# A transformer layer with a routed mixture: the second batch's rows are sent two at a time among the expert blocks' transfers

## The reference, cut to what matters

```
x = layernorm(x + attention(x))                     # 2 batches of 1024 tokens, width 128, 16 heads
logits = router(x)                                  # 8 experts
top_logits, idx = top_k(logits, 2); scores = softmax(top_logits)
for e in range(8):
    a, g = split(x_rep @ w1[e].T, 2)                # width 352 each
    he = silu(a) * g @ w2[e].T
    out = out + where(expert_ids == e, he, 0)
combined = (out * scores).reshape(N, 2, 128).sum(1)
x = layernorm(x + combined)
```

## Time and profile before

| what | value |
|---|---|
| median of 3 runs | 865.77 us (865.43 to 865.95) |
| the profiled execution | 863.55 us |
| its span, first to last instruction | 861.8 us |
| PE busy | 765.6 us, 89% |
| ACT busy | 687.8 us, 80% |
| POOL busy | 673.9 us, 78% |
| DVE busy | 537.6 us, 62% |
| mean granted TensorE clock | 0.967 |

### The profile page before, as it was taken

One profiled execution on the slowest core, in us unless ns is written; L12 is line 12 of the kernel. 1 busy time (PEld: TensorE's weight loads), 2 busy tenths in 40 slices (PEclk: granted clock), 3 DMA queues, 4 the chain that ended last, 5 costly groups with the idle time before them and its releaser, 6 DMA issues. The chain is left out here.

```text
span 861.8 us, 22282 instructions
## 1 busy us (share of the span) xinstructions
PE 765.6 (89%) x9183; PEld 525.2 (61%) x9183; DVE 537.6 (62%) x907; ACT 687.8 (80%) x854; POOL 673.9 (78%) x430
## 2 busy tenths in 40 slices
PE   2889999999999999999999999999988657839991
PEld 0346565666666666666666666666655446729990
DVE  6856667666666676666866667766653167515673
ACT  3899999998989898999999898989889755214452
POOL 5799888888888797888898789999999962554441
PEclk9999999999999999999999999999999987959996
DMA  5603064303031211213040404031200041121212
GB/s 174 150 2 75 5 139 82 78 2 78 8 72 27 53 39 41 54 27 75 5 108 5 112 2 111 14 99 39 48 11 17 11 117 44 36 71 51 79 40 86
DMA packets 43138, 49.30 MB, mean 57 GB/s; under 512 B 6785, under 2 KB 27655, under 8 KB 42912
## 3 DMA queue, kind: packets, MB, share of 16 engines
q1 hardware_dynamic: 39872, 43.31, 20.4%
q0 software_dynamic: 2496, 4.24, 1.5%
q10 hardware_dynamic: 672, 0.33, 0.2%
HBM read 14.28 MB, written 9.25 MB: 27 GB/s over the span
## 5 line engine op out<-in xcount | busy, mean ns | idle before, releaser
L882 POOL TENSOR_TENSOR pl<-p,ph 128x1024 f16<-128x1024 f32 x256 | 541.0, 2130 | 70.2 <-ACT ph L784 69.6
L944 DVE TENSOR_REDUCE mx<-mps 128x1 f32<-128x1024 f32 x249 | 303.8, 1220 | 133.7 <-PE mps L619 131.6
L783 ACT ACTIVATE p<-sps,escale 128x1024 f32<-128x1024 f32 x256 | 286.3, 1118 | 51.2 <-PE sps L599 45.6
L784 ACT ACTIVATE ph<-sps,escale 128x1024 f16<-128x1024 f32 x256 | 284.9, 1113 | 0.0
L694 PE MATMUL pair_bank<-v,ph 128*128 128x65 f16 x2048 | 214.7, 193 | 16.8 <-POOL pl L882 15.2
L694 PEld LDWEIGHTS pair_bank<-v,ph 128*128 128x128 f16 x2048 | 190.4, 96 | 55.7 <-POOL pl L882 25.2
L696 PE MATMUL pair_bank<-v,ph 128*128 128x64 f16 x2048 | 214.4, 195 | 0.0
L698 PE MATMUL pair_bank<-v,pl 128*128 128x65 f16 x2048 | 214.0, 192 | 0.0
L696 PEld LDWEIGHTS pair_bank<-v,ph 128*128 128x128 f16 x2048 | 190.0, 97 | 27.6
L598 PE MATMUL sps<-q_hh,k_hl 128*128 128x512 f16 x512 | 194.1, 379 | 1.8 <-ACT ph L784 1.5
L599 PE MATMUL sps<-q_lm,k_h 65*128 65x512 f16 x512 | 194.7, 380 | 0.0
(11 more groups left out here) (256 smaller groups left out, 966.8 us busy)
## 6 DMA issues: line engine op xcount, KB each, us to landing
q_hh<-hi SPq DMA_DIRECT2D x60, 128.0 KB, 2.3
q_lm<-lo SPq DMA_DIRECT2D x30, 128.0 KB, 2.4
k_h<-hi SPq DMA_DIRECT2D x30, 128.0 KB, 2.5
k_hl<-hi SPq DMA_DIRECT2D x29, 128.0 KB, 2.6
k_hl<-lo SPq DMA_DIRECT2D x29, 128.0 KB, 2.6
sorted<-pad SPq DMA_DIRECT2D x1, 2990.0 KB, 16.8
xb<-sorted SPq DMA_DIRECT2D x46, 65.0 KB, 1.8
v<-in_w1T SPq DMA_DIRECT2D x8, 352.0 KB, 3.5
```

The lines of the kernel that those rows point to most:

```text
L783: nc.scalar.activation(p32[:, n % 4, :], sps[:, n % 2, :], ACT.Exp, bias=EXP_BIAS, scale=escale[:, 0:1])
L784: nc.scalar.activation(ph[:, n % 4, :], sps[:, n % 2, :], ACT.Exp, bias=EXP_BIAS, scale=escale[:, 0:1]).then_inc(s_exp, 1)
L882: nc.gpsimd.tensor_tensor(pl[:, n % 4, :], p32[:, n % 4, :], ph[:, n % 4, :], ALU.subtract).then_inc(s_subp, 1)
L944: nc.vector.tensor_reduce(mx[:, i // TB, i % TB:i % TB + 1], src, AX.X, ALU.max).then_inc(s_mx, 1)
```

## The change: where GpSimd sends the second batch's rows

Before, all 16 sends stand in one run between the transfers home of blocks 7 and 8. Now the waits stay where they were, and each of the iterations 8 to 15 issues two sends ahead of its own wait for `yb` and its transfer home. The number of sends, their sources, addresses and semaphores are the same, and so is the wait of SyncE for all 16.

```diff
-            def send_rows():
-                pool.wait_ge(s_ids, 2)
-                pool.wait_ge(s_rows1, 4)
-                f.wait_part(pool, 1, "weight", 0)
-                f.wait_part(pool, 1, "where", 1)
-                for n in range(2 * TB):
-                    send_row(nc, f, io, 1, n)
-
             for i in range(B * NBB):
                 if i == LATE_SEND:
-                    send_rows()
+                    pool.wait_ge(s_ids, 2)
+                    pool.wait_ge(s_rows1, 4)
+                    f.wait_part(pool, 1, "weight", 0)
+                    f.wait_part(pool, 1, "where", 1)
+                if LATE_SEND <= i < LATE_SEND + TB:
+                    send_row(nc, f, io, 1, 2 * (i - LATE_SEND))
+                    send_row(nc, f, io, 1, 2 * (i - LATE_SEND) + 1)
                 pool.wait_ge(s_yb, i + 1)
                 nc.gpsimd.indirect_dma_start(
```

## The result

| | before | changed |
|---|---|---|
| median of 19 runs each, run in turns, us | 865.24 (864.26 to 866.13) | 863.83 (861.79 to 864.53) |
| profiled execution, us | 863.55 | 864.21 |
| its span, us | 861.8 | 862.5 |

The ratio is 0.9979, with a 95% interval of 0.9973 to 0.9986: 1.4 us faster, where 10.5 us had been forecast.

A forecast was written before the change was run, and what follows sets the result against it. Bound: engines stopped at 744 to 770 us because TensorE's done-word came late beside 16 sends. Block 23 earlier, -12.5, half clock behind it, +2.0: -10.5 us from the median 865.77 gives 855.3 us; range 853.0 to 873.

The forecast's parts named there:

- the price of a pair: Delay that two adjacent sends cost the engines, blocks 8 to 15: taken as some 1 us, from 0.2 to 4 us.
- the slack: Engines could reach block 23 at about 766, its data at 776: 10 us spare, 1.25 us for each of eight pairs.
- the stop: Engines quiet at 744 to 770 us, TensorE's done-word arriving late beside 16 sends; about 23 us lost in all.
- the lone send and the four in a row: Sends in attention and at the mixture's start, whose hand-overs showed 0.2 us or nothing, read as a low price.
- The place of the last send: Behind seven transfers home, the last send starts at 772.0 instead of 763.10, 8.9 us later, covered by the engines' stop.
- the cap of 12.5 us: Largest gain: block 23 can be transposed at 776.1, once its sends are done, in place of 788.6.
- The half clock of 2.0 us behind block 23: TensorE waits at block 23, so the half clock paid before it is paid behind it: +2.0 us.
- the last sentence of the prediction: If the granted clock falls during the pairs, not only before block 23, the gain is smaller than handing-over alone gives.
- That silence lets the word through: When a finished block is late, GpSimd waits for `yb` and falls silent, which lets TensorE's done-word reach the other engines.
- B: Rival, chance 0.30: any dense string of indirect DMAs, homes included, blocks TensorE's word; 7.4 us a block, slower, 872 us.
- A: Rival, chance 0.18: each pair holds TensorE's word for much of its length; gain about 4 us, 861.8 us.
- C: Rival, chance 0.08: the stop has another cause and lasts as long as before; 5.6 us slower, 871 us.

The follow-up runs named there:

- the repeated run: The changed kernel, unchanged, run again on another chip where hand-overs are on time: 853.79 us beside 844.0 for the kernel before, ratio 1.0119.

## Why the prediction was wrong, step by step

**The step that failed is the price of a pair**, "some 1 us a pair", taken at the low end of 0.2 to 4 us. Against the undisturbed 22.08 us from block 8 to block 23 the changed kernel took 43.82: 21.7 us lost, 2.7 us for each of eight pairs beyond what the pipeline covers, where the slack allowed 1.25. The kernel before had lost 22.85. So spreading the sends saved 1.1 us of the stop, not 12.5. The sum had taken each pair as a piece of its own, parted from the next by a transfer home. In the trace GpSimd issues that transfer 0.30 us behind the sends, like another send, and the pairs join into strings of 9, 9 and 7 DMAs. The upper end of the range for a pair (3 to 4 us, "as long as it lasts and a little beyond") was the right size, if one counts by pairs at all; the stops come one to a string. What had argued for the low end was the lone send and the four in a row. The lone send's 0.20 us should have weighed the other way, as a sign that the disturbance can begin at one DMA.

**The place of the last send** came out as worked out, 28.2 us behind the first, where nothing is late. In the result it was 33.2 (778.79 - 745.60): 28.2 and the excess of the two waits over the ordinary 0.30 us, 2.54 and 2.43. From it to SyncE's first fetch (781.12) it was 2.33 us, 2.3 forecast. Where nothing is late, block 23's transpose follows block 8's product by 32.75 us (776.80 - 744.05), 32.4 in the forecast (776.1 - 743.67), so the cap of 12.5 us was worked out rightly (as a time of the median it is 853.3 us, not the 853.0 of the range). In the result the cap was lower, since the last send came later, and it didn't bind: block 23 was in SBUF by about 783, TensorE there at 789.07.

**The half clock of 2.0 us behind block 23** is right where TensorE does wait there for long: 75.4 us to the end (75.1 in the repeated run), against 73.4 without the wait. In the result there was no wait and nothing to pay (73.4); the half clock was paid in each of the stops instead, as the last sentence of the prediction feared.

**That silence lets the word through** fits part of the trace, but isn't shown. GpSimd's string ends at 755.55, VectorE starts at 755.77 and ScalarE at 757.24; after 769.63 ScalarE starts at 771.21; after 781.05 both do, at 782.31 and 782.40. Against a strict form of it stands 768.35, a release within the string, like 758.54 in the earlier trace rows. And each later string begins with prompt hand-overs, 0.04 us at 762.04 (VectorE) and 763.19 (ScalarE), and again at 776.01 and 777.01, 3.7 to 4.8 us behind the string's first DMA; the late ones come after that. This fits the prompt hand-over of the earlier trace rows, and suggests that a short string does little, but the string of pairs and homes wasn't short. Since two or three pairs get by in each string before ScalarE has a product ready, the wait for `yb` makes GpSimd's own gap, too late and only three times.

**The rivals.** B, any dense string, had the mechanism that the trace looks most like, though not its count of one block to each triple: VectorE's wait of 7.43 us up to 755.77 spans a home (752.00) and the sends on both sides of it. Its price was too high: 4.54 us a block from 8 to 15, not 7.4, which is under its own point of decision of 5.4, and so the kernel isn't slower. A comes nearest in time (861.8 forecast, 863.83 measured). Neither is shown against the other; a string here always holds both kinds, and the kernels that would have told a string of homes from a string of sends ran only where neither holds anything. C is out as it stood, because the one stop didn't keep its place and length; that GpSimd's DMAs make it is supported by the new pattern of stops, which follows GpSimd's strings. No run removed the sends where the stop is, so it is argued and not shown.

**What no step of the prediction had seen**: that the 21 us aren't the kernel's alone. On the six chips of the later runs the unchanged kernel runs without them. The changed one was run on two of them and does the opposite there, 9.8 us slower, by the very step (the last send 8.9 us later forecast, 9.1 measured) that was thought to be covered. The cover was the stop.

The Trainium skill, SBUF — State Buffer, section "Who interferes with whom", says that DMA never contends with a compute engine; it says so of the ports to SBUF, and says nothing of hand-overs. Read as the prediction read it, it agrees with the on-time traces (0.04 us in nearly all hand-overs; the traces of four of the six chips have the 16 sends, those of the other two 18 transfers home in a row). The two traces of the first comparison don't agree with that reading (up to 17.6 us late before; after, up to 6.9 us late, in a wait of 7.43).

What differs between the two places stays open. Which chip made the first comparison isn't known, so it can be a seventh or one of the six. The difference can lie in the chip, in how the program was placed on it, or in what else ran beside it.

## What to carry to other kernels

A step that is late by much while its data are long there is worth a second look at where it was measured: run the unchanged kernel on another chip first, and compare hand-overs beside isolated DMAs in the two traces, where one of them differed here (0.20 and 0.04 us). Spreading the DMAs over time bought 1.1 us here where they came with the stop, and cost the full delay of the last one, 9 us, where nothing was disturbed. The transfers home between the pairs parted nothing, since the queue didn't have to wait for them. Before spacing out what one queue issues, ask which fetch waits for its last element, and whether the queue can still make up its arrears afterwards.

## What was unexpected of the hardware

- The same program takes 865.2 us in one place and 843.7 to 844.1 on six chips, steadily in each (all 19 runs of the one lie between 864.26 and 866.13; of the others none is above 846.21). Between the two traces the difference lies where TensorE's hand-overs are late, beside 16 indirect DMAs of GpSimd (21.25 us from block 8 to block 23).
- Where they are late, breaking 16 sends into pairs changes how long each hand-over is late (17.6 us at most before, some 7 after), and hardly the time lost by them (22.85 and 21.7 us).
- GpSimd issues a plain transfer of the same rows in some 0.54 us (16 in 8.58 us), an indirect one in 1.27 us. Where nothing is late the difference is worth 2 us in this kernel (842.08 and 844.12), since TensorE waits only 1.56 us for the last send.
